# Splitting six PSUM banks two to four between exponential scores and row maxima, with row maxima taken two heads at a time

## The chip, the cores and the metric

The kernel runs on one core of one Trainium2 chip. The metric is the device time of the whole program in microseconds (us). Its engines are PE (matmuls; PEld is its weight load), DVE (vector), ACT (scalar), POOL and SP, each with its own instruction stream, tied together by semaphores.

## The reference

```python
# x: (1, 2048, 128) f32; 16 heads of 8, latent width 64; all operands f32
c_kv   = x @ W_dkv.T
q_lat  = einsum('bqhd,hdl->bhql', (x @ W_dq.T @ W_uq.T).reshape(B, T, 16, 8), k_eff)
attn   = softmax(where(causal, einsum('bhql,bkl->bhqk', q_lat, c_kv) / sqrt(8), -inf))
y      = einsum('bhql,hld->bqhd', einsum('bhqk,bkl->bhql', attn, c_kv), v_eff)
x1     = layernorm(x + y)
# mixture of experts: 2 groups of tokens, 8 experts, top 2, at most 80 tokens each
h      = relu(einsum('egch,ehf->egcf', expert_in, wi)); expert_out = einsum('egcf,efh->egch', h, wo)
out    = layernorm(x1 + combine(expert_out))
```

Causal attention over 2048 tokens and 16 heads comes first and takes most of the time; the experts' work is laid between its pieces.

## The kernel before

**Units and steps.** The queries are cut into 4 supers of 512 and the heads into 4 groups of 4 (HG), which makes 16 units. A unit of super s has 4(s+1) steps (L80): a step takes 128 keys against the 512 queries for the unit's four heads. There are 160 steps. For each head of a step PE computes a transposed tile of scores (keys on the partitions, L1089) into a bank of PSUM, ACT takes the exponential out of it into SBUF (L662), and two steps later PE multiplies the four heads' exponentials with the values into the bank `acc` (`attn_v`, L1106, eight short-weight matmuls a step). The last four steps of a unit lie on the diagonal: they are 512, 384, 256 and 128 queries wide and have one more small matmul (L1093), which adds the mask.

**Maxima.** The exponentials need each row's maximum beforehand. So for a later unit PE also computes tiles the other way round, with queries on the partitions ("items", L1067), and DVE takes the maximum of each. An item is (query tile qt, head h, 512 keys c), in the order of L100. Off the diagonal it is 512 wide and DVE uses TENSOR_REDUCE (L789); the item on the diagonal is (qt+1)*128 wide and DVE adds a mask and takes the maximum in one instruction (L794), followed by a short read of its accumulator. `max_rows` (L797) joins the parts, PE turns the result (L1074), ACT copies it (L638) and a DMA puts it into rows of qT.

**Banks.** PSUM has eight banks. Three (`scT`) are a ring for the exponentials' scores, three (`sc`) a ring for the items, one is `acc`, one `ms` is for turns and the experts. From step WIDE = 140 on there are no items left; then all six ring banks serve the scores, two tiles to one exponential (L660). Score n waits until the exponential that last used its bank is done (L1087); item i waits until item i-3 has been reduced (L1065).

**The order of work.** `woven()` (L119) gives each step its items. It goes backwards from the last item and fills steps up to a limit of work (`item_work`, 60 plus the width, L113; limits 2400 and, for the first 20 steps, 3000), so that a unit's items are done LEAD = 5 steps before the unit begins. A step's items are cut into four gaps. PE's order in one step is: gap 0's items, score 0, gap 1's items, score 1, `attn_v` of two steps before (unless that is a unit's first step, when it comes after gap 3), gap 2's items, score 2, gap 3's items, score 3, and then the step's tasks. All engines execute their own instructions in order. DVE takes the items of a step before that step's other work, and fills some waits with items of the next step.

```
per_step[b].insert(0, i)
...
if early and gap == 2:
    attn_v(due)
for i in gaps[gap]:
    scores_for_max(i)
if b < NSTEP:
    scores(b, gap)
```

**Tasks** (`SCHEDULE`) are the unit's copy of its result `keep_y` (ACT, L673, after the exponentials of the next unit's second step), the turns, layer norms, the router and the experts (`expert_h` L1191, `expert_o` L1197). PE's part of a task stands after score 3 of its step.

Of the kernel before, what the change touches and what calls it, by code (L numbers as in the profile page):

```python
# [26 lines left out]
P = 128  # L27
# [3 lines left out]
QUERIES = 512  # L31
SUPERS = T // QUERIES
TILES = T // P
QT = QUERIES // P
HG = 4
# [6 lines left out]
MROW = 126  # L42
VC = HD + 1
PRING = 12
SRING = 3
AHEAD = 1
EARLY = 16
LEAD = 5
# [3 lines left out]
BIG = -1e38  # L52
# [16 lines left out]
F32, BF16, U32 = mybir.dt.float32, mybir.dt.bfloat16, mybir.dt.uint32  # L69
ALU = mybir.AluOpType  # L70
ACT = mybir.ActivationFunctionType
AX = mybir.AxisListType
# [3 lines left out]
def super_of(u):  # L76
    return u // GROUPS
# [19 lines left out]

def max_items(u):

    return [(qt, h, c) for qt in range(QT) for h in range(HG) for c in range(super_of(u) + 1)]  # L100


ITEMS_BEFORE = [0]
# [4 lines left out]
def max_step(u):  # L108

    return max(0, FIRST[u] - LEAD - 1)  # L110


def item_work(i):  # L113

    u, qt, _, c = ALL_ITEMS[i]
    return 60 + (QUERIES if c < super_of(u) else (qt + 1) * P)


def woven():  # L119

    per_step = [[] for _ in STEPS]
    i, b, work = len(ALL_ITEMS) - 1, FIRST[UNITS - 1], 0
    while i >= ITEMS_BEFORE[AHEAD] + EARLY:
        last = max_step(ALL_ITEMS[i][0])
        limit = ITEM_WORK if b >= RUSH else RUSH_WORK
        if b > last or work + item_work(i) > limit:
            b, work = (b - 1, 0)
            assert b >= 0  # L130
            continue
        per_step[b].insert(0, i)
        work += item_work(i)
        i -= 1
    return [[row[len(row) * gap // 4:len(row) * (gap + 1) // 4] for gap in range(4)] for row in per_step]


# [7 lines left out]
WIDE = max_step(UNITS - 1) + 2  # L145


def score_bank(n):

    return n % SRING if n < HG * WIDE else n % (2 * SRING)  # L150


def used_before(n):

    return max((m for m in range(max(0, n - 4 * SRING), n) if score_bank(m) == score_bank(n)), default=None)


def schedule():
# [87 lines left out]
def program(nc, x_d, wdq_d, wuq_d, wdkv_d, wuk_d, wuv_d, wo_d, router_d, wi_d, wo2_d, out_d):  # L246
    ctx = ExitStack()
    with ctx:
# [12 lines left out]
        qT = [sb(f"qT{i}", [P, HEADS, QUERIES], BF16) for i in range(2)]  # L261
# [47 lines left out]
        causal = sb("causal", [P, QUERIES])  # L309
# [3 lines left out]
        unused = [sb(f"unused{i}", [P, QUERIES], BF16) for i in range(2)]  # L313
        part_max = [sb(f"part_max{i}", [P, QT * HG, SUPERS]) for i in range(2)]
# [38 lines left out]
        back2 = sb("back2", [P, MT, C])  # L353
        ein = back2[:, 0:ST, :]

        ring = ctx.enter_context(nc.psum_tensor("ring", [P, 2 * SRING, QUERIES], F32))
        scT = [ring[:, i, :] for i in range(SRING)]
        sc = [ring[:, SRING + i, :] for i in range(SRING)]
        acc = ctx.enter_context(nc.psum_tensor("acc", [P, QUERIES], F32))
        ms = ctx.enter_context(nc.psum_tensor("ms", [P, QUERIES], F32))  # L360
        BANKS = [*scT, *sc, acc[:, :], ms[:, :]]

        s_w = sem("s_w")
        s_router = sem("s_router")
# [18 lines left out]
        v_kept = sem("v_kept")  # L383
        kq_first = [sem(f"kq_first{g}") for g in range(GROUPS)]
        kq_in = [sem(f"kq_in{i}") for i in range(SUPERS)]
        sc_made = sem("sc_made")
        sc_used = sem("sc_used")
# [33 lines left out]
        def turn_bank(task):  # L421
            return BANKS[bank_of(TURN[task])]

# [301 lines left out]
        def _(dve):  # L725
            made = [0]
            items = [ITEMS_BEFORE[AHEAD], 0]
            may_fill = [False]

            def next_item():  # L730
                row_max(items[0])
                items[0] += 1

            def link(ins):

# [47 lines left out]

            def row_max(i):
                u, qt, h, c = ALL_ITEMS[i]
                dve.wait_ge(sc_made, i + 1)
                dst = part_max[u % 2][:, qt * HG + h, c:c + 1]
                if c < super_of(u):
                    nc.vector.tensor_reduce(dst, sc[i % SRING][:, :], AX.X, ALU.max).then_inc(sc_used, 1)  # L789
                else:  # L790
                    w = (qt + 1) * P
                    if i >= 2:
                        dve.wait_ge(sc_used, i - 1)
                    nc.vector.tensor_tensor_reduce(unused[i % 2][:, 0:w], sc[i % SRING][:, 0:w], causal[:, QUERIES - w:QUERIES], 1.0, 3 * BIG,  # L794
                                                   ALU.add, ALU.max, dst).then_inc(sc_used, 1)

            def max_rows(u):  # L797

# [14 lines left out]
            for u in range(AHEAD):  # L813
                for i in range(ITEMS_BEFORE[u], ITEMS_BEFORE[u + 1]):
                    row_max(i)
                max_rows(u)
            for _ in range(EARLY):
                next_item()

            def moments(rows, kind, k):  # L820
# [192 lines left out]
        def _(pe):  # L1013
# [42 lines left out]
            def scores_for_max(i):  # L1056

                u, qt, h, c = ALL_ITEMS[i]
                s, head = super_of(u), u % GROUPS * HG + h
                if i == ITEMS_BEFORE[u] and s == 0:  # L1060
                    pe.wait_ge(kq_first[u], 16 * 2 * PARTS)
                if i == ITEMS_BEFORE[u] and s and u == s * GROUPS:
                    pe.wait_ge(kq_in[s], 16 * 2 * PARTS)
                if i >= SRING:
                    pe.wait_ge(sc_used, i - SRING + 1)  # L1065
                w = QUERIES if c < s else (qt + 1) * P
                nc.tensor.matmul(sc[i % SRING][:, 0:w], qT[s % 2][0:MROW, head, qt * P:(qt + 1) * P],  # L1067
                                 kT[0:MROW, head, c * QUERIES:c * QUERIES + w], start=True, stop=True).then_inc(sc_made, 1)

            def turn_max(u, bank):  # L1070
# [170 lines left out]
```

## Time and profile before

| what | us |
|---|---|
| median of 3 runs | 589.88 |
| lowest and highest of them | 589.47, 592.38 |
| the profiled execution's own time | 590.35 |
| its span in the profile | 588.5 |
| PE busy | 525.7 (89%) |
| DVE busy | 442.9 (75%) |
| ACT busy | 354.1 (60%) |

The span is what the trace covers; 1.85 us of the profiled execution lie around it. A matmul's row is longer than the time it takes from its successor, since the array is a pipeline: matmuls of one kind follow each other at a shorter pitch than their duration. So PE's "busy" says little about how full PE is; the pitch of its rows says it. Attention runs from about 50 to 522 us; steps with items end at about 482.

### The profile page before, as it was taken

The page shows a single profiled execution, that of the slowest core. Times are in us where ns is not written, and L with a number is a line of the kernel's source. Part 1 is how long each engine was busy: PE and PEld are TensorE (multiplying, and loading weights), DVE is VectorE, ACT ScalarE, POOL GpSimd, SP SyncE. Part 2 cuts the span into 40 slices and gives each one's busy share as a digit, 9 for nine tenths or more (in the row PEclk, how much of TensorE's full clock was granted, in tenths as well). Part 3 has the DMA queues.
Part 4 walks back from the last instruction along what each step waited for, and adds up shares of the span by engine and source line. Part 5 has one row for each costly group of instructions (what it writes and reads, how often), then busy time and mean ns, then how long its engine had stood idle before and what let it go on. Part 6 is the DMA issues. An engine that isn't in the chain of part 4 may idle for free.

```text
span 588.5 us, 10326 instructions
## 1 busy us (share of the span) xinstructions
PE 525.7 (89%) x3491; PEld 217.9 (37%) x3491; DVE 442.9 (75%) x1300; ACT 354.1 (60%) x719; POOL 63.2 (11%) x64
## 2 busy tenths in 40 slices
PE   4967999899999998989989999989999999955991
PEld 2523333233333333224545333333223222223891
DVE  3687999898888979976757878988888872445616
ACT  0613556656667765664765777667777779934231
POOL 9400000000000000450000460000000000000031
PEclk9966999999999999998999999999999999985996
DMA  3379991300000300010000160000000000000024
GB/s 87 120 225 232 200 279 51 58 2 2 2 1 2 82 1 1 29 64 6 1 13 1 37 48 3 1 3 0 1 2 2 1 2 10 19 9 1 0 41 55
DMA packets 25410, 24.90 MB, mean 42 GB/s; under 512 B 2314, under 2 KB 22668, under 8 KB 25356
## 3 DMA queue, kind: packets, MB, share of 16 engines
q1 hardware_dynamic: 21660, 20.42, 13.7%
q0 software_dynamic: 1280, 2.62, 3.8%
q10 hardware_dynamic: 2416, 1.18, 0.7%
q8 instruction: 28, 0.46, 0.3%
q14 instruction: 26, 0.21, 0.1%
HBM read 16.81 MB, written 7.28 MB: 41 GB/s over the span
## 4 chain that ended last, share of the span: by engine, by line
PE 59%; issue 20%; DVE 11%; DMA 3%; POOL 3%; ACT 2%; SPq 0%; ACTq 0%; DVEq 0%; POOLq 0%
PE acc L1106 16%; PE ring L1067 15%; PE ring L1089 13%; DVE part_max L789 3%; POOL exp_in L579 3%; DVE unused L794 2%; PE ring L1093 2%; PE ms L1170 2%; DMA qT<-maxT 1%; PE ms L1197 1%; PE ms L1191 1%; PE ring L1184 1%; PE ring L1197 1%; PE ring L1191 1%; DVE x L865 1%
## 5 line engine op out<-in xcount | busy, mean ns | idle before, releaser
L662 ACT ACTIVATE probs<-ring 128x512 f32<-128x512 f32 (+3 forms) x560 | 268.5, 536 | 136.4 <-PE ring L1093 74.0
L789 DVE TENSOR_REDUCE part_max<-ring 128x1 f32<-128x512 f32 x384 | 254.4, 686 | 45.1 <-PE ring L1067 42.1
L1067 PE MATMUL ring<-kT,qT 126*128 126x512 bf16 (+3 forms) x640 | 221.6, 360 | 10.0 <-DVE part_max L794 4.5
L1089 PE MATMUL ring<-qT,kT 128*128 128x512 bf16 (+3 forms) x640 | 214.5, 352 | 4.0 <-DMA qT<-maxT 3.2
L1106 PE MATMUL acc<-probs,v 128*9 128x512 f32 (+3 forms) x1280 | 147.6, 533 | 0.9 <-ACT yT L673 0.9
L794 DVE CUSTOM_DVE_ANT_0 unused<-ring,causal 128x128 bf16<-128x128 f32 (+3 forms) x256 | 120.3, 483 | 20.3 <-PE ring L1067 18.0
L1067 PEld LDWEIGHTS ring<-kT,qT 126*128 126x128 bf16 x640 | 61.9, 98 | 178.7 <-DVE part_max L789 102.5
L1089 PEld LDWEIGHTS ring<-qT,kT 128*128 128x128 bf16 x640 | 61.9, 99 | 46.7 <-ACT probs L660 15.7
L1093 PE MATMUL ring<-later,ident 128*128 128x128 bf16 x256 | 55.4, 221 | 0.0
L1106 PEld LDWEIGHTS acc<-probs,v 128*9 128x9 f32 x1280 | 19.0, 88 | 50.6 <-issue 25.7
L660 ACT ACTIVATE probs<-ring 128x1024 f32<-128x1024 f32 (+3 forms) x40 | 33.2, 900 | 2.8 <-issue 1.6
L1093 PEld LDWEIGHTS ring<-later,ident 128*128 128x128 bf16 x256 | 25.6, 100 | 19.8 <-issue 0.4
L603 POOL TENSOR_TENSOR res<-res,x 128x512 f32<-128x512 f32 x3 | 3.8, 1268 | 225.3 <-DVEq L845 225.3
L794 DVE DVE_READ_ACCUMULATOR2_ANT part_max<- 128x1 f32 x256 | 21.3, 83 | 0.0
L593 POOL DMA_INDIRECT back<-exp_out,slot_out x16 | 15.3, 954 | 51.1 <-DMA exp_out<-x 46.5
L854 DVE SCALAR_TENSOR_TENSOR nt<-rs 128x2 f32<-128x2 f32 (+1 forms) x12 | 1.9, 160 | 22.7 <-ACT rs L685 22.6
L579 POOL DMA_INDIRECT exp_in<-x,slot_in x16 | 15.7, 982 | 24.1 <-DVE slot_in L926 19.5
L683 ACT ACTIVATE lnv<-mv,eps 128x2 f32<-128x2 f32 (+1 forms) x12 | 3.7, 305 | 23.9 <-DVE mv L827 23.9
L606 POOL IOTA kT<- 128x640 f32 x1 | 0.7, 665 | 141.1 <-PE ring L1093 141.1
L593 POOL DMA_INDIRECT x<-exp_out,slot_out x8 | 7.6, 954 | 70.9 <-DMA exp_out<-x 68.7
L638 ACT ACTIVATE maxT<-ms 8x512 bf16<-8x512 bf16 x16 | 9.3, 579 | 9.3 <-PE ms L1074 9.0
L559 POOL MEMSET kT<- 64x4096 uint32 x4 | 13.9, 3509 | 0.1
(179 smaller groups left out, 341.1 us busy)
## 6 DMA issues: line engine op xcount, KB each, us to landing
kT<-parts_k SPq DMA_DIRECT2D x9, 384.0 KB
qT<-parts_q SPq DMA_DIRECT2D x9, 384.0 KB
wi<-in_L_ffn_wi SPq DMA_DIRECT2D x1, 2048.0 KB, 18.5
parts_k<-wi SPq DMA_DIRECT2D x3, 384.0 KB, 3.6
parts_q<-wi SPq DMA_DIRECT2D x3, 384.0 KB, 4.8
kT<-parts_k SPq DMA_DIRECT2D x12, 96.0 KB
qT<-parts_q SPq DMA_DIRECT2D x12, 96.0 KB
x<-in_L_attn_x ACTq DMA_DIRECT2D x4, 256.0 KB, 4.4
```

What stands on the lines that cost most here:

```text
L559: nc.gpsimd.memset(rows, one_pair).then_inc(s_rows, 1)
L579: pool.indirect_dma_start(exp_in_d[:, :], bass.IndirectOffsetOnAxis(slot_in[:, n:n + 1], 0), x1[:, g * MT + n % MT, :], None).then_inc(sca ...
L593: pool.indirect_dma_start(dst, None, exp_out_d[g][:, :], bass.IndirectOffsetOnAxis(slot_out[:, n:n + 1], 0)).then_inc(gathered[PIECES * g ...
L660: nc.scalar.activation(probs[:, at:at + 2, 0:width], ring[:, bank:bank + 2, 0:width], ACT.Exp).then_inc(exp_done, 2)
L662: nc.scalar.activation(probs[:, at, 0:width], ring[:, bank, 0:width], ACT.Exp).then_inc(exp_done, 1)
L789: nc.vector.tensor_reduce(dst, sc[i % SRING][:, :], AX.X, ALU.max).then_inc(sc_used, 1)
L794: nc.vector.tensor_tensor_reduce(unused[i % 2][:, 0:w], sc[i % SRING][:, 0:w], causal[:, QUERIES - w:QUERIES], 1.0, 3 * BIG, ALU.add, ALU. ...
L1067: nc.tensor.matmul(sc[i % SRING][:, 0:w], qT[s % 2][0:MROW, head, qt * P:(qt + 1) * P], kT[0:MROW, head, c * QUERIES:c * QUERIES + w], sta ...
L1089: ins = nc.tensor.matmul(bank[:, 0:QUERIES - off], kT[:, head, j * P:(j + 1) * P], qT[s % 2][:, head, off:QUERIES], start=True, stop=True, ...
L1093: ins = nc.tensor.matmul(bank[:, 0:P], ident16[:, :], later16[:, :], start=False, stop=True, skip_group_check=True)
L1106: ins = nc.tensor.matmul(acc[32 * h:32 * h + VC, off:QUERIES], v[:, j, head, :], probs[:, (HG * b + h) % PRING, 0:QUERIES - off], start=(j ...
L1170: ins = nc.tensor.matmul(bank[:, 0:n], x1[:, g * MT + i, :], hot[i][:, part * QUERIES:part * QUERIES + n], start=(i == 0), stop=(i == MT - 1))
```

## The change

```diff
-SRING = 3
+SRING = 2
+MRING = 4
+PAIR = 2
 
 def max_items(u):
-    return [(qt, h, c) for qt in range(QT) for h in range(HG) for c in range(super_of(u) + 1)]
+    return [(qt, h + i, c) for qt in range(QT) for h in range(0, HG, PAIR) for c in range(super_of(u) + 1) for i in range(PAIR)]
 
@@ woven
-        per_step[b].insert(0, i)
-        work += item_work(i)
-        i -= 1
+        per_step[b] = [i - 1, i] + per_step[b]
+        work += PAIR * item_work(i)
+        i -= PAIR
 
 def score_bank(n):
-    return n % SRING if n < HG * WIDE else n % (2 * SRING)
+    return n % SRING if n < HG * WIDE else n % (SRING + MRING)
 
@@ banks
-        ring = ctx.enter_context(nc.psum_tensor("ring", [P, 2 * SRING, QUERIES], F32))
-        scT = [ring[:, i, :] for i in range(SRING)]
-        sc = [ring[:, SRING + i, :] for i in range(SRING)]
+        ring = ctx.enter_context(nc.psum_tensor("ring", [P, SRING + MRING, QUERIES], F32))
+        scT = [ring[:, i, :] for i in (0, 1, 5)]
+        sc = [ring[:, SRING + i, :] for i in range(MRING)]
 
@@ row_max, on DVE
-                dve.wait_ge(sc_made, i + 1)
-                dst = part_max[u % 2][:, qt * HG + h, c:c + 1]
                 if c < super_of(u):
-                    nc.vector.tensor_reduce(dst, sc[i % SRING][:, :], AX.X, ALU.max).then_inc(sc_used, 1)
+                    dve.wait_ge(sc_made, i + PAIR)
+                    at = SRING + i % MRING
+                    nc.vector.tensor_reduce(part_max[u % 2][:, qt * HG + h:qt * HG + h + PAIR, c], ring[:, at:at + PAIR, :],
+                                            AX.X, ALU.max).then_inc(sc_used, PAIR)
+                    return PAIR
                 else:
+                    dve.wait_ge(sc_made, i + 1)
+                    dst = part_max[u % 2][:, qt * HG + h, c:c + 1]
                     w = (qt + 1) * P
                     if i >= 2:
                         dve.wait_ge(sc_used, i - 1)
 
@@ scores_for_max, on PE
-                if i >= SRING:
-                    pe.wait_ge(sc_used, i - SRING + 1)
+                if i >= MRING:
+                    pe.wait_ge(sc_used, i - MRING + 1)
+                if i == MRING - 1:
+
+                    pe.wait_ge(v_kept, SUPERS)
```

Not shown: `i % SRING` becomes `i % MRING` where items are written and read, `next_item` counts by what `row_max` returns, `used_before` looks back 2 * (SRING + MRING) = 12 scores as before, and the early loop of DVE runs until the same 16 items are done. The third V tile of the start (`scT[2]`) lies in ring bank 5, which is now also the items' fourth bank; the new wait of item 3 is for that.

The exponentials' scores have two banks instead of three until step 140, the items four instead of three. Two heads' off-diagonal items of the same qt and c stand next to each other, in adjacent banks, and one TENSOR_REDUCE of 2 x 512 takes both maxima; it waits for both tiles and frees both banks when it ends. The diagonal items keep an instruction each. `woven()` places items in twos, so that a step has an even number of them: evaluated, the new plan has 2, 4, 6 or 8 items in a step, and none in steps 0, 3, 11 to 13, 19, 43, 44, 55, 56, 91, 92, 107, 108, 123 and 124; the old one has 3 or more in nearly every step below 139. With R for an off-diagonal item, 1 to 4 for a diagonal one of that many 128 columns, and | between the gaps, the pattern of steps 113 to 124 is:

```
step  before     after
113   2|R|R|R    R|R2|2|RR
114   2|R|R|R2   R|RR|R|22
115   R|R|R|3    R|R|R|R
116   R|R|R|3    R|R|3|3
117   R|R|R|3    R|R|R|R
118   R|R|R|3    R|R|3|3
119   R|R|R|4    R|R|R|R
120   R|R|R|4    R|R|4|4
121   R|R|R|4    R|R|R|R
122   R|R|R|4    R|R|4|4
123   |R|R|R     |||
124   1|R|R|R    |||
127   1|R|R|R    R|RR|R|11
```

## Rows read from the trace of the kernel before

**Rows 1.** The page: busy time of the engines, and two of its costliest groups
```profile
PE 525.7 (89%) x3491; PEld 217.9 (37%) x3491; DVE 442.9 (75%) x1300; ACT 354.1 (60%) x719; POOL 63.2 (11%) x64
...
L789 DVE TENSOR_REDUCE part_max<-ring 128x1 f32<-128x512 f32 x384 | 254.4, 686 | 45.1 <-PE ring L1067 42.1
L1067 PE MATMUL ring<-kT,qT 126*128 126x512 bf16 (+3 forms) x640 | 221.6, 360 | 10.0 <-DVE part_max L794 4.5
```

**Rows 2.** The chain of work that ended last, 405 to 450 us, by line
```profile
by line: PE acc L1106 32.5%; PE ring L1067 32.3%; PE ring L1089 26.6%; DVE part_max L789 4.5%; PE ring L1093 1.6%; DVE unused L794 0.9%; PE ms L1074 0.9%; issue 0.8%; DVE max L810 0.2%; DVE part_max L794 0.0%
```

**Rows 3.** The timeline of one regular step, 117: start us, us, instruction, idle before
```profile
417.30 0.39 PE L1067 MATMUL ring<-kT,qT 126*128 126x512 bf16 x1
...
417.52 0.38 PE L1089 MATMUL ring<-qT,kT 128*128 128x512 bf16 x1
...
417.72 0.69 DVE L789 TENSOR_REDUCE part_max<-ring 128x1 f32<-128x512 f32 x1 [0.41 <-PE ring L1067]
...
417.91 0.38 PE L1089 MATMUL ring<-qT,kT 128*128 128x512 bf16 x1
...
417.94 2.07 ACT L662 ACTIVATE probs<-ring 128x512 f32<-128x512 f32 x4 [0.71 <-PE ring L1089]
...
418.34 0.38 PE L1089 MATMUL ring<-qT,kT 128*128 128x512 bf16 x1
...
418.78 0.38 PE L1089 MATMUL ring<-qT,kT 128*128 128x512 bf16 x1
...
419.09 1.05 PE L1106 MATMUL acc<-probs,v 128*9 128x512 f32 x8
...
420.07 0.39 PE L1067 MATMUL ring<-kT,qT 126*128 126x512 bf16 x1
```

**Rows 4.** Groups by form, whole span: count, busy us, mean ns, idle before
```profile
L662 ACT ACTIVATE probs<-ring 128x512 f32<-128x512 f32 x392 | 208.8, 601 | 84.3 <-PE ring L1089 58.8 <-PE ring L1093 23.1 <-PE acc L1106 1.2
...
L794 DVE CUSTOM_DVE_ANT_0 unused<-ring,causal 128x512 bf16<-128x512 f32 x64 | 42.8, 683 | 4.3 <-PE ring L1067 3.9 <-DVE res L840 0.3
...
L662 ACT ACTIVATE probs<-ring 128x384 f32<-128x384 f32 x56 | 26.1, 496 | 14.8 <-PE ring L1093 14.5
...
L794 DVE CUSTOM_DVE_ANT_0 unused<-ring,causal 128x128 bf16<-128x128 f32 x64 | 17.6, 283 | 6.9 <-PE ring L1067 6.3 <-DVE res L840 0.3
```

**Rows 5.** The timeline where a unit begins, steps 113 and 114
```profile
409.85 0.38 PE L1089 MATMUL ring<-qT,kT 128*128 128x512 bf16 x1
410.00 0.60 ACT L673 ACTIVATE yT<-acc 128x512 f32<-128x512 f32 x1
...
410.42 1.88 DVE L789 TENSOR_REDUCE part_max<-ring 128x1 f32<-128x512 f32 x3
410.44 0.38 PE L1089 MATMUL ring<-qT,kT 128*128 128x512 bf16 x1
410.48 2.08 ACT L662 ACTIVATE probs<-ring 128x512 f32<-128x512 f32 x4
...
411.16 0.10 PEld L1067 LDWEIGHTS ring<-kT,qT 126*128 126x128 bf16 x1 [0.51 <-DVE part_max L789]
...
411.28 0.38 PE L1089 MATMUL ring<-qT,kT 128*128 128x512 bf16 x1
```

**Rows 6.** The timeline of a step with an expert's matmuls behind score 3
```profile
300.40 0.38 PE L1089 MATMUL ring<-qT,kT 128*128 128x512 bf16 x1
...
300.62 1.01 PE L1191 MATMUL ms<-einT,wi 128*128 128x80 f32 x8
...
301.53 0.38 PE L1089 MATMUL ring<-qT,kT 128*128 128x512 bf16 x1
```

**Rows 7.** Who waited for whom, whole span: us in total, times, longest
```profile
PEld ring L1067 <- DVE part_max L789: 102.5, 180, 1.4
...
PE ring L1067 <- DVE part_max L794: 4.5, 8, 2.6
...
PE ring L1067 <- DVE part_max L789: 3.7, 10, 0.9
...
PE ms L1164 <- DMA back<-exp_in: 2.7, 1, 2.7
```

**Rows 8.** Stretches: us, busy us of the engines, granted clock, DMA share, GB/s
```profile
60.00:100.00 40.00, 38.02 (x295) 15.51 (x294) 37.88 (x129) 23.20 (x58) 0.00 (x0) 1.00 0.72 178
...
250.00:300.00 50.00, 47.18 (x321) 20.77 (x318) 34.69 (x83) 31.20 (x65) 8.73 (x9) 0.97 0.08 24
...
400.00:450.00 50.00, 49.44 (x327) 15.91 (x327) 42.39 (x96) 35.91 (x78) 0.00 (x0) 1.00 0.00 1
```

More of the change, by code:

```diff
@@ L148, in score_bank @@
 def score_bank(n):
-    return n % SRING if n < HG * WIDE else n % (2 * SRING)
+    return n % SRING if n < HG * WIDE else n % (SRING + MRING)
 def used_before(n):
-    return max((m for m in range(max(0, n - 4 * SRING), n) if score_bank(m) == score_bank(n)), default=None)
+    return max((m for m in range(max(0, n - 2 * (SRING + MRING)), n) if score_bank(m) == score_bank(n)), default=None)
 def schedule():
@@ L354, in program @@
         ein = back2[:, 0:ST, :]
-        ring = ctx.enter_context(nc.psum_tensor("ring", [P, 2 * SRING, QUERIES], F32))
-        scT = [ring[:, i, :] for i in range(SRING)]
-        sc = [ring[:, SRING + i, :] for i in range(SRING)]
+        ring = ctx.enter_context(nc.psum_tensor("ring", [P, SRING + MRING, QUERIES], F32))
+        scT = [ring[:, i, :] for i in (0, 1, 5)]
+        sc = [ring[:, SRING + i, :] for i in range(MRING)]
         acc = ctx.enter_context(nc.psum_tensor("acc", [P, QUERIES], F32))
         ms = ctx.enter_context(nc.psum_tensor("ms", [P, QUERIES], F32))
-        BANKS = [*scT, *sc, acc[:, :], ms[:, :]]
+        BANKS = [*scT[0:SRING], *sc, acc[:, :], ms[:, :]]
         s_w = sem("s_w")
@@ L730, in next_item @@
             def next_item():
-                row_max(items[0])
-                items[0] += 1
+                items[0] += row_max(items[0])
             def link(ins):
@@ L793, in row_max @@
                         dve.wait_ge(sc_used, i - 1)
-                    nc.vector.tensor_tensor_reduce(unused[i % 2][:, 0:w], sc[i % SRING][:, 0:w], causal[:, QUERIES - w:QUERIES], 1.0, 3 * BIG,
+                    nc.vector.tensor_tensor_reduce(unused[i % 2][:, 0:w], sc[i % MRING][:, 0:w], causal[:, QUERIES - w:QUERIES], 1.0, 3 * BIG,
                                                    ALU.add, ALU.max, dst).then_inc(sc_used, 1)
+                    return 1
             def max_rows(u):
@@ L816, in _ @@
                 max_rows(u)
-            for _ in range(EARLY):
+            while items[0] < ITEMS_BEFORE[AHEAD] + EARLY:
                 next_item()
@@ L1063, in scores_for_max @@
                     pe.wait_ge(kq_in[s], 16 * 2 * PARTS)
-                if i >= SRING:
-                    pe.wait_ge(sc_used, i - SRING + 1)
+                if i >= MRING:
+                    pe.wait_ge(sc_used, i - MRING + 1)
+                if i == MRING - 1:
+                    pe.wait_ge(v_kept, SUPERS)
                 w = QUERIES if c < s else (qt + 1) * P
-                nc.tensor.matmul(sc[i % SRING][:, 0:w], qT[s % 2][0:MROW, head, qt * P:(qt + 1) * P],
+                nc.tensor.matmul(sc[i % MRING][:, 0:w], qT[s % 2][0:MROW, head, qt * P:(qt + 1) * P],
                                  kT[0:MROW, head, c * QUERIES:c * QUERIES + w], start=True, stop=True).then_inc(sc_made, 1)
```

## The prediction

> **What bounds the kernel now.** I read the page first: PE is busy 89% of the span, DVE 75%, ACT 60% [rows 1]. A full PE row can hide waits, so the chain comes next. Over one whole unit it runs through PE for over nine tenths and through DVE's maxima for 4.5 + 0.9 = 5.4% [rows 2]: PE streams, and DVE is seldom late. Then the timeline of one step [rows 3]. The matmul before a score starts at 417.30 and the score at 417.52, so a 512-column matmul takes 0.22 of PE though its row says 0.38. The four scores between two attn_v's (call them S1 to S4; they are scores 2 and 3 of one step and 0 and 1 of the next, and I call this a cluster) start at 417.52, 417.91, 418.34 and 418.78; attn_v begins at 419.09 and the next step's first item at 420.07. The step is 2.77 us, with no hole for PE. The ring of three score banks is what makes this possible, and the row of ACT shows by how much.
>
> **The score ring, three banks to two.** Score n may now start when exponential n-2 is done, not n-3. The first exponential starts at 417.94, 0.42 after S1 starts, and lasts 0.60 [rows 3, 4]: it ends at 418.54. Four of them take 2.07, so they follow each other at (2.07 - 0.60)/3 = 0.49. From the end of a releasing instruction to PE's next start there is 0.05: of three maxima that take 1.88 from 410.42 at 0.69 for the last, the first ends at 411.11, and the load that waited for it starts at 411.16 [rows 5]. I take 0.06 with the matmul behind the load. So S3 can't start before 418.60, and it started at 418.34: a stall of 0.26. Exponential 2 starts at 418.43 and ends at 419.03, so S4 can't start before 419.09; shifted with S3 it would come at 419.04: 0.05 more. A regular cluster with four wide items costs about 0.3, and S1 and S2 cost nothing, since attn_v's 0.98 stands before them. The same sum for other clusters of the new plan, always (0.42 + 0.60 + 0.06 = 1.08) against what stands between S1 and S3 at 0.22 a wide matmul and 0.054 for each 128 columns of a narrow one:
> - 46 clusters below step 139 between two full-width steps, 4 to 6 items, no task behind score 3: 30 x 0.28 + 9 x 0.23 + 7 x 0.10 = 11.2 us.
> - 5 such with only 2 or 3 items, next to an empty step: 0.68 each, 3.4 us. 5 between two empty steps (S1 to S4 would take 0.65, and need 1.56; the maxima's turn fills some 0.25): 0.61 each, 3.0 us.
> - 38 with diagonal steps: their exponentials are shorter (0.50 at 384 [rows 4]) and the masks fill: 0.18 each, 6.8 us.
> - Some 45 with a task of PE behind score 3. An expert's eight matmuls put 1.13 between S2 and S3 [rows 6] (300.40 to 301.53), above the 0.6 that is missing at most: nothing. If these tasks were not there, they would pay as the others do.
> Together 24 us. Bounds: with no release delay at all S3's stall is 0.20, which makes 18; with every stall also delaying what comes behind, 30.
>
> **At a unit's start** attn_v is missing in the middle of one step and ACT's copy of the result (L673) stands between exponentials. There S5 started at 410.44, and the exponential two before it ends at 410.48 + 0.60 = 411.08 [rows 5]: 0.70 short instead of 0.28. Eleven units pay this 0.42 more: 5 us; from 2 (the old stall for DVE at 411.16 lies in the same place) to 8.
>
> **The pairs on DVE.** 384 instructions become 192 [rows 1]. Off two singles at a pitch of 0.60 (1.88 for three), 1.29 us, one of 1024 elements is not in the trace. Between the L794 rows 384 more columns cost 683 - 283 = 400 ns [rows 4], 0.133 for 128, so 512 more cost 0.53 and a pair lasts 0.69 + 0.53 = 1.22; from 0.69 (the second half free) to 1.37 (nothing saved). At 1.22 DVE gets back 0.07 a pair, 13 us of work, of which PE feels what it waited for DVE. PE's own rows show 4.5 + 3.7 = 8 us of waits for maxima [rows 7]; the chain's 5.4% of 45 us is 2.4 a unit, 27 us over eleven units if all of it were regained. I take 8, the waits that are seen, with 5 and 28 as ends. The 102.5 us of loads that waited [rows 7] are not a price: they lie beside attn_v.
>
> **The pairs on PE.** A pair must be whole before it is reduced, and frees two banks only at its end. With four banks item i waits for item i-4. In the pattern R|R|R|R a pair lies within gaps 0 and 1, or 2 and 3, and nothing is late. In R|RR|R|11, R|RR|R|22 and 2|2R|R|33 a pair has its first tile before attn_v and its second behind. From attn_v's end: the second tile starts, its reduce starts 0.42 later [rows 3] (417.30 to 417.72), lasts 1.22, and PE hears 0.05 after: 1.69. PE wants that bank for the first item of the next step after item, score, two narrow items, score: 0.22 + 0.22 + 0.11 + 0.22 = 0.77. That is 0.9 of stall, 0.8 with 22. The score stall of the same cluster (0.3) is inside it. The new plan has 31 such steps; 12 have a task behind score 3 and are reached late enough (together some 2.5 us), the other 19 add about 0.65 each, 12.3; three of them are a unit's third step, where attn_v comes elsewhere: -1.6. Together 13 us, from 6 (pairs nearer 0.69) to 22. The Trainium skill, in Perfetto Trace Analysis, Optimizing Scalar/DVE Operations, says that where DVE is not saturated but makes others wait, breaking instructions up lets work end sooner. By that rule the merging costs time even where it saves DVE work, as in the 13 us here. The same section says that grouping helps an engine that is saturated; by that the merging would bring up to 13 us instead. The trace, with DVE at 42.39 of 50 us [rows 8] and PE seldom waiting for it, agrees with the first.
>
> **Edits at nothing.** A diagonal maximum behind a pair now waits for the pair's end (0.05 to 0.1, some 90 times): DVE has 15% free, and would cost up to 9 us without it. The wait of item 3 for the V copies lies at the start, where DVE still splits k and q and the fourth item waited for it anyway. After step 140 the banks are as before. The 16 empty steps are paid above; their items make others fuller, and in the first 20 steps, where DVE is busy 37.88 of 40 us [rows 8], they leave DVE idle and then press it: 0 to 4 us.
>
> **The sum.** 24 + 5 + 13 - 8 = +34. On the profiled execution (590.35, of which 588.5 are the span) that is 624.4; it lies 0.5 above the median of the runs, so I say 624.
>
> **Rivals.** (A) The straddling pairs cost little, because DVE takes them early enough or the stall falls into the score stall: 24 + 5 - 8 = +21, 611. For: DVE's idle time before L789 is 45 us, almost all of it for PE [rows 1], so it starts at once. Against: the 0.77 against 1.69. (B) DVE decides: each maximum saved shortens the step wherever DVE sets the pace, and PE's queue swallows the score stalls. Then -13 us, 577. For: DVE's 37.88 of 40 in the early stage. It decides from the point where DVE's work for a step is longer than PE's; for four wide items it is 4 x 0.60 = 2.4 against 2.77 [rows 3], so hardly anywhere. (C) The third bank is slack: ACT's exponentials keep up and the kernel stays at 590 +- 3. Against: exponential n-2 ends after score n starts, in the row itself. (D) The clock. So far the granted clock is 1.00 (2.4 GHz) in the stages with items, and 0.97 in 250 to 300 [rows 8], where PE once stood for 2.7 us [rows 7]. If the new regular stalls of 0.3 in 3 us pulled it down in one step of ten, 14 steps would take up to 2.8 more: 39 on top, 663. The stage of 60 to 100, with PE waiting for DVE time and again, kept 1.00. The Trainium skill, TensorE: Matmul & The Clock Gate, A second HAM failure mode, tells of a kernel whose short idles at its PSUM banks made the clock go up and down; the trace does not show it for waits of this length.
>
> **How the numbers follow.** Forecast 0.60, A 0.24, D 0.05, B 0.05, C 0.06. The range takes the forecast's bounds, from 590 + 18 + 2 + 6 - 20 = 596 to 590 + 30 + 8 + 22 - 5 = 645; all low ends together are unlikely, so 603 to 645, which holds A and leaves out B, C and D. A measurement of this kernel tells about 0.5% from no change. Slower by more: 0.60 + 0.24 + 0.05 and a small part of C, 0.90; faster 0.05; the same 0.05.
>
> **What would show it.** The regular step at about 3.07 us instead of 2.77 where items are R|R|R|R, with PE's load for L1089 released by ACT's exponential; steps with R|RR|R|11 at about 3.8 with the load for L1067 released by L789; L789 192 times at 1.2 us; DVE's busy time lower by some 13 us; ACT's busy time unchanged. The span from step 140 on should be unchanged. The prediction is wrong if S3 starts less than 0.42 + 0.60 after S1 with full-width tiles, if L1067 does not wait in straddling steps, or if the clock falls between 60 and 480 us.

## The result and the profile after

The changed kernel takes 644.39 us (median of 4 runs, 642.21 to 646.77) beside 589.69 for the kernel before on the same chip: a ratio of 1.0931, 95% interval 1.0907 to 1.0956. It is slower, by 54.7 us where +34 was forecast; 644.39 lies just inside the range's upper end of 645. The profiled execution took 644.41, with a span of 642.7.

The page of the changed kernel, against [rows 1]:

```profile
PE 538.7 (84%) x3491; PEld 214.8 (33%) x3491; DVE 439.0 (68%) x1108; ACT 364.6 (57%) x719; POOL 63.1 (10%) x64
...
L790 DVE TENSOR_REDUCE part_max<-ring 128x2 f32<-128x1024 f32 x192 | 232.2, 1223 | 91.0 <-PE ring L1076 89.9
L1076 PE MATMUL ring<-kT,qT 126*128 126x512 bf16 (+3 forms) x640 | 211.5, 360 | 31.2 <-DVE part_max L790 26.3
L1098 PE MATMUL ring<-qT,kT 128*128 128x512 bf16 (+3 forms) x640 | 216.6, 355 | 18.9 <-ACT probs L664 11.2
```

PE and ACT execute as many instructions as before, and DVE fewer. PE's and ACT's busy time is 13.0 and 10.5 us longer all the same, in part because rows that follow each other at once overlap and fewer do so now: four exponentials of 0.60 took 2.07 in a run before, and take 2.17. What grew is waiting in both directions: DVE stood 91.0 us before its maxima where it was 45.1, and PE 26.3 us before an item, for DVE's pairs, where it was 3.7. Two engines that wait more for each other, with the same work, have lost slack between them. The waits say the same, against [rows 7] (first the changed kernel, then the rows of the kernel before that [rows 7] has not):

```profile
PEld ring L1076 <- DVE part_max L790: 77.4, 99, 1.6
PEld ring L1098 <- ACT probs L664: 76.3, 155, 2.1
...
PE ring L1076 <- DVE part_max L790: 26.3, 44, 1.2
...
PE ms L1153 <- DVE x L871: 7.5, 3, 2.6
...
PE ms L1083 <- DVE max L816: 6.1, 5, 2.8
```

```profile
PEld ring L1089 <- ACT probs L662: 4.0, 10, 0.9
...
PE ms L1144 <- DVE x L865: 3.6, 3, 1.2
...
PE ms L1074 <- DVE max L810: 2.5, 3, 1.9
```

The second row of the changed kernel is the score ring: the load for a score waits for an exponential 155 times, where it did so 10 times. Its last two have nothing to do with banks: PE waits up to 2.8 us for a layer norm (`x`) and for the finished maxima (`max`), in all 13.6 us where it was 6.1. The chain of waits from 450 to 500 us, about one unit like that of [rows 2], has the maxima at 15.8% where they had 4.5, and ACT at 6.1% where it had no entry:

```profile
by line: PE acc L1115 26.0%; PE ring L1098 22.6%; PE ring L1076 21.2%; DVE part_max L790 15.8%; ACT probs L664 6.1%; issue 5.8%; ACTq L645 1.3%; ACT maxT L640 0.9%; PE ring L1102 0.9%; DVE unused L799 0.5%; DVE part_max L799 0.3%; DVEq L788
```

**A regular step**, R|R|R|R, on the timeline; this answers [rows 3]:

```profile
457.42 1.04 PE L1115 MATMUL acc<-probs,v 128*9 128x512 f32 x8
...
458.62 0.38 PE L1098 MATMUL ring<-qT,kT 128*128 128x512 bf16 x1
...
459.04 2.17 ACT L664 ACTIVATE probs<-ring 128x512 f32<-128x512 f32 x4 [0.87 <-PE ring L1098]
...
459.69 0.10 PEld L1098 LDWEIGHTS ring<-qT,kT 128*128 128x128 bf16 x1 [0.53 <-ACT probs L664]
459.69 0.39 PE L1098 MATMUL ring<-qT,kT 128*128 128x512 bf16 x1
...
460.18 0.39 PE L1098 MATMUL ring<-qT,kT 128*128 128x512 bf16 x1
...
460.50 1.05 PE L1115 MATMUL acc<-probs,v 128*9 128x512 f32 x8
```

S1 starts at 458.62, S3 at 459.69: 1.07 apart, where the forecast had 1.08. S4 follows at the exponentials' pitch, and attn_v comes 3.08 after the last (forecast 3.07, before 2.77). **A crowded step** of the pattern R|RR|R|11:

```profile
442.50 0.38 PE L1076 MATMUL ring<-kT,qT 126*128 126x512 bf16 x1
...
442.60 2.36 DVE L790 TENSOR_REDUCE part_max<-ring 128x2 f32<-128x1024 f32 x2 [0.37 <-PE ring L1076]
...
443.88 0.39 PE L1076 MATMUL ring<-kT,qT 126*128 126x512 bf16 x1 [0.67 <-DVE part_max L790]
...
444.31 0.83 PE L1115 MATMUL acc<-probs,v 128*9 128x384 f32 x8
...
445.58 1.23 DVE L790 TENSOR_REDUCE part_max<-ring 128x2 f32<-128x1024 f32 x1 [0.62 <-PE ring L1076]
...
446.86 0.39 PE L1076 MATMUL ring<-kT,qT 126*128 126x512 bf16 x1 [1.05 <-DVE part_max L790]
```

The pair that straddles attn_v begins at 445.58, and the item that needs its bank waits 1.05 us for the end of it. That wait was foreseen (0.9). The one at 443.88 was not: two pairs stand in a row on DVE, and PE reaches the bank of the first while it is still being reduced. From its first item to that of the next step this one takes 4.36 us, and 1.72 of them are the two waits. It is not the forecast's own case, though: it is the last step of a unit, its own scores are 128 wide and take PE little time, so PE comes to each bank early. Steps 95, 111 and 127 are of this kind. In step 36 (R|RR|R|22, scores 512 wide) the trace has the one foreseen wait, 0.62 us long at 182.44, and the step takes 4.06.

Where in the kernel does the time go? By the start of a step's first score in the two traces, the changed kernel is 0.7 us ahead at step 4, then behind by 3.9 at step 20, 19.9 at step 48, 34.1 at step 96 and 53.5 at step 140, and it stays at 53.5 to the end. So nearly all of it comes before the last step with items, some 0.4 us a step from step 20 on. (The new plan has 4, 6, 8 or 10 items in a step that has any: 10 in steps 1 and 4, and in none only 2.)

### The profile page after: what moved, and what is told of

The parts are those of the page before. It is cut to its first block, busy times and chain, and to the rows that moved or that the text cites. A ratio compares the mean times of both kernels' runs of the same rounds, so it can differ in the third digit from the quotient of the medians.

```text
span 642.7 us, 10324 instructions
## 1 busy us (share of the span) xinstructions
PE 538.7 (84%) x3491; PEld 214.8 (33%) x3491; DVE 439.0 (68%) x1108; ACT 364.6 (57%) x719; POOL 63.1 (10%) x64
## 4 chain that ended last, share of the span: by engine, by line
PE 49%; issue 23%; DVE 16%; ACT 5%; DMA 3%; POOL 3%; ACTq 1%; SPq 0%; DVEq 0%; POOLq 0%
PE acc L1115 14%; PE ring L1098 12%; PE ring L1076 11%; DVE part_max L790 9%; POOL exp_in L581 2%; ACT probs L664 2%; PE ms L1179 2%; DMA qT<-maxT 1%; PE ms L1206 1%; PE ms L1200 1%; DVE unused L799 1%; PE ring L1193 1%; PE ring L1102 1%; PE ring L1206 1%; PE ring L1200 1%
## 5 line engine op out<-in xcount | busy, mean ns | idle before, releaser
L664 ACT ACTIVATE probs<-ring 128x512 f32<-128x512 f32 (+3 forms) x560 | 277.9, 532 | 173.2 <-PE ring L1102 88.6
L790 DVE TENSOR_REDUCE part_max<-ring 128x2 f32<-128x1024 f32 x192 | 232.2, 1223 | 91.0 <-PE ring L1076 89.9
L1076 PE MATMUL ring<-kT,qT 126*128 126x512 bf16 (+3 forms) x640 | 211.5, 360 | 31.2 <-DVE part_max L790 26.3
L799 DVE CUSTOM_DVE_ANT_0 unused<-ring,causal 128x128 bf16<-128x128 f32 (+3 forms) x256 | 115.0, 488 | 29.2 <-PE ring L1076 17.7
L1076 PEld LDWEIGHTS ring<-kT,qT 126*128 126x128 bf16 x640 | 59.9, 99 | 169.5 <-DVE part_max L790 77.4
L860 DVE SCALAR_TENSOR_TENSOR nt<-rs 128x2 f32<-128x2 f32 (+1 forms) x12 | 1.9, 160 | 23.6 <-ACT rs L687 23.5
## 6 DMA issues: line engine op xcount, KB each, us to landing
wi<-in_L_ffn_wi SPq DMA_DIRECT2D x1, 2048.0 KB, 19.9
```

Source lines behind the costliest of these rows:

```text
L664: nc.scalar.activation(probs[:, at, 0:width], ring[:, bank, 0:width], ACT.Exp).then_inc(exp_done, 1)
L790: nc.vector.tensor_reduce(part_max[u % 2][:, qt * HG + h:qt * HG + h + PAIR, c], ring[:, at:at + PAIR, :], AX.X, ALU.max).then_inc(sc_used ...
L1076: nc.tensor.matmul(sc[i % MRING][:, 0:w], qT[s % 2][0:MROW, head, qt * P:(qt + 1) * P], kT[0:MROW, head, c * QUERIES:c * QUERIES + w], sta ...
```

## The experiments

Differences of medians are given in us. The interval of each ratio reaches 0.2 to 0.5% to either side, 1 to 3 us, and the runs come from three chips, on which the kernel before took 589.6, 589.5 and 588.8. So a difference between two of these kernels is known to 3 or 4 us.

**1. Banks, plan and merging apart.** In the first kernel only the banks are new (2 and 4), with the old order and one maximum at a time:

```diff
-    return [(qt, h + i, c) for qt in range(QT) for h in range(0, HG, PAIR) for c in range(super_of(u) + 1) for i in range(PAIR)]
+    return [(qt, h, c) for qt in range(QT) for h in range(HG) for c in range(super_of(u) + 1)]
-        per_step[b] = [i - 1, i] + per_step[b]
+        per_step[b].insert(0, i)
@@ row_max
-                    dve.wait_ge(sc_made, i + PAIR)
-                    at = SRING + i % MRING
-                    nc.vector.tensor_reduce(part_max[u % 2][:, qt * HG + h:qt * HG + h + PAIR, c], ring[:, at:at + PAIR, :],
-                                            AX.X, ALU.max).then_inc(sc_used, PAIR)
-                    return PAIR
+                    dve.wait_ge(sc_made, i + 1)
+                    nc.vector.tensor_reduce(part_max[u % 2][:, qt * HG + h, c:c + 1], sc[i % MRING][:, :], AX.X, ALU.max).then_inc(sc_used, 1)
+                    return 1
```

> Only the banks are split two to four; the plan of the items and their single maxima are those of the kernel before. Theory (the score ring is the main cost, with the pairs that straddle attn_v second): +24 for the clusters of the old plan, +5 at unit starts, little back from a fourth item bank: 615 to 620 us, the regular step 3.07 us instead of 2.77. Rival (the third score bank is slack, the merging costs all): 588 to 592. Second rival (the score ring costs the whole of it): 640 or more.

Measured: 605.98, ratio 1.0278 (1.0230 to 1.0326), +16. That is between the theory and its first rival, and neither had it: the third score bank is not slack, but it costs 16 of the 29 expected.

The second has only the new order and plan, with three and three banks and single maxima (the changed kernel with the lines below and the diff above in `row_max`, and without the new wait of item 3):

```diff
-SRING = 2
-MRING = 4
+SRING = 3
+MRING = 3
-        scT = [ring[:, i, :] for i in (0, 1, 5)]
+        scT = [ring[:, i, :] for i in range(3)]
```

> Only the order and the plan of the items in twos, with banks three and three and a maximum for each item. Theory: the empty steps cost little while there are three score banks, 590 to 598 us. Rival (the plan's empty and crowded steps are where the 20 us come from by which the changed kernel is slower than forecast): 605 to 612.

Measured: 608.01, 1.0323 (1.0277 to 1.0369), +18, as the rival had it. Its regular step is nearly as before (2.82 from one attn_v to the next). Its waits show a part of the 18 us: PE waits for DVE 35 times where [rows 7] has 10, 6.8 us more in all:

```profile
PE ring L1071 <- DVE part_max L789: 10.5, 35, 1.1
```

Another part lies in the 16 empty steps. There PE has only scores and attn_v, and even with three banks the load for a score waits for an exponential 25 times, 15.4 us in all by the trace, where the kernel before has 8 such waits, 2.6 us, in all its steps below 139. Some of that lies beside attn_v, so it is not a price, and the 18 us were not divided further.

The third is the changed kernel with nothing undone but the merging, that is, with the diff in `row_max` above and nothing else.

> The changed kernel with each off-diagonal maximum taken by an instruction of its own; banks and plan stay as changed. Theory: the straddling pairs fall away and no item waits for its neighbour: 644 less 13 to 25, so 619 to 631; a step with R|RR|R|11 at about 3.2 us instead of 3.6 to 4.4. Rival (the merging saves DVE time and is not what costs): 644 to 655.

Measured: 612.57, 1.0399 (1.0356 to 1.0442), +23, below the 619 to 631 of the theory: the merging costs more than I thought. Of the 54.7 us, banks and plan together make 23 and **the merging 31.8**. In this kernel's waits PE's own row for the maxima is as small as before:

```profile
PE ring L1074 <- DVE part_max L789: 3.9, 15, 0.8
```

The plan costs 18 with banks three and three and only 6.6 more (612.57 - 605.98) with two and four, where PE's waits for DVE fall from 10.5 to 3.9. Read the other way, the banks cost 16 in the old plan and 4.6 (612.57 - 608.01) in the new one. That the fourth item bank is what cushions the crowded plan fits those rows. It may also be that the stalls of the one hide in those of the other. No run had 2 and 3 banks with the new plan, so both are argued and not shown.

**2. Is the fourth item bank of use in the old plan?** Two score banks, three item banks and one idle, with the old order and single maxima (`MRING = 3` and `SPARE = 1` in the first kernel).

> Two banks for the scores as changed, but three for the items as before (the eighth bank idle), plan and single maxima as before: the score ring alone. The split of banks cost 16 where 29 had been forecast. Theory (the fourth item bank gives some of the difference back, as fewer waits for DVE): 609 to 615 us. Rival (the fourth item bank is worth nothing and the score ring costs only 16): 604 to 607.

Measured: 606.56, 1.0291 (1.0261 to 1.0321), 0.6 from the first kernel, which is the rival's result. No worth of the fourth item bank can be told there; the 17 us are the score ring alone. Its timeline has the stall in its pure form:

```profile
429.58 1.04 PE L1111 MATMUL acc<-probs,v 128*9 128x512 f32 x8
...
431.85 0.10 PEld L1094 LDWEIGHTS ring<-qT,kT 128*128 128x128 bf16 x1 [0.58 <-ACT probs L665]
...
432.33 0.10 PEld L1094 LDWEIGHTS ring<-qT,kT 128*128 128x128 bf16 x1 [0.37 <-ACT probs L665]
...
432.66 1.05 PE L1111 MATMUL acc<-probs,v 128*9 128x512 f32 x8
```

Again 3.08 from attn_v to attn_v, with DVE in no way involved.

**3. The straddling pairs.** If the merging costs time because a pair lies on both sides of attn_v, keeping it whole must give that back. First with both tiles behind attn_v, R|R|RR|11:

```diff
+    cut = [len(row) * gap // 4 for gap in range(5)]
+    if cut[2] % PAIR:
+        u, _, _, c = ALL_ITEMS[row[cut[2]]]
+        if c < super_of(u):
+            cut[2] -= 1
+    return [row[cut[gap]:cut[gap + 1]] for gap in range(4)]
```

> The changed kernel with one cut moved: an off-diagonal pair is never divided by attn_v (R|RR|R|11 becomes R|R|RR|11). Theory: the 19 steps in question regain about 0.65 us each and those with a task a little: 644 less 10 to 20, so 624 to 634. Rival (a pair costs by its length wherever it stands): 642 to 646.

Measured: 638.23, 1.0829 (1.0784 to 1.0875), only 6.2 below the changed kernel: less than the theory's 10 to 20, and more than the rival's nothing. Then with both ahead of it, R|RRR||11, so that attn_v covers the reduction:

```diff
-            cut[2] -= 1
+            cut[2] += 1
+            cut[3] = max(cut[2], cut[3])
```

> The changed kernel with the divided pair put whole ahead of attn_v (R|RR|R|11 becomes R|RRR||11), so that it is reduced beside attn_v. The run before put it whole behind attn_v and gained 6 us. Theory (what costs is that the pair ends 1.7 us behind attn_v while the next step's first item wants its bank): most crowded steps go from 3.6-4.4 to 3.0-3.3 us, 644 less 12 to 20, so 624 to 632. Rival (a pair costs by being two tiles long wherever it stands, DVE then being late for the next one): 636 to 642.

Measured: 634.23, 1.0776 (1.0737 to 1.0816), 10.2 below, between the theory's 12 and the rival's 8. PE's waits for pairs fall from 26.3 to

```profile
PE ring L1087 <- DVE part_max L801: 17.3, 33, 1.2
```

So the straddling is real and costs about what was forecast (13, of which 10 come back). But two thirds of the 31.8 are somewhere else.

**4. The pairs as fills.** `link()` on DVE puts an item's maximum between two short instructions that depend on each other. A single maximum there is 0.69 long and waits for one tile; a pair is 1.22 long and waits for two. The changed kernel's DVE in the last instructions of a layer norm, on which PE's turn (L1153) waits:

```profile
419.89 0.16 DVE L860 SCALAR_TENSOR_TENSOR nt<-rs 128x4 f32<-128x4 f32 x1
419.96 1.22 DVE L790 TENSOR_REDUCE part_max<-ring 128x2 f32<-128x1024 f32 x1
421.10 0.16 DVE L861 TENSOR_TENSOR nt<-nt,var 128x4 f32<-128x4 f32 x1
421.90 1.23 DVE L790 TENSOR_REDUCE part_max<-ring 128x2 f32<-128x1024 f32 x1 [0.65 <-PE ring L1076]
423.04 0.15 DVE L862 SCALAR_TENSOR_TENSOR rs<-nt,rs 128x4 f32<-128x4 f32 x1
423.23 1.12 DVE L871 TENSOR_SCALAR x<-res,mv,rs 128x128 f32<-128x128 f32 x4
```

L861 done, DVE sits 0.65 us in a fill whose second tile PE hasn't made, though L862 could run. In the experiment only diagonal items, which kept an instruction each, may fill:

```diff
-                if may_fill[0] and items[0] < items[1]:
+                u, _, _, c = ALL_ITEMS[min(items[0], len(ALL_ITEMS) - 1)]
+                if may_fill[0] and items[0] < items[1] and c == super_of(u):
```

> The changed kernel in which DVE fills the waits of its chained small operations with a diagonal item only, never with a pair. Theory (each filled wait now takes 1.22 us and waits for two tiles, so the chains of the layer norms end late and PE's turns with them): steps 57, 58, 105 and 106 regain 1 to 1.5 us each, 644 less 4 to 8, so 636 to 640. Rival (the fills cost nothing, the chain's PE turns were late anyway): 643 to 646.

Measured: 635.00, 1.0789 (1.0750 to 1.0829), 9.4 below the changed kernel where 4 to 8 were expected. The same instructions:

```profile
414.64 0.16 DVE L861 SCALAR_TENSOR_TENSOR nt<-rs 128x4 f32<-128x4 f32 x1
414.83 0.16 DVE L862 TENSOR_TENSOR nt<-nt,var 128x4 f32<-128x4 f32 x1
415.02 0.16 DVE L863 SCALAR_TENSOR_TENSOR rs<-nt,rs 128x4 f32<-128x4 f32 x1
415.22 1.11 DVE L872 TENSOR_SCALAR x<-res,mv,rs 128x128 f32<-128x128 f32 x4
```

and PE's waits for that output:

```profile
PE ms L1154 <- DVE x L872: 0.2, 1, 0.2
```

From L861 (L860 in the other) to the start of the norm's output at L872 it is 0.58 us instead of 3.34, and of the 7.5 us that PE waited 0.2 are left. A part of the gain is the clock. In the changed kernel PE stood 2.58, 2.40 and 2.48 us before its three turns of a norm's output, at 142.09, 250.81 and 424.49. The three stretches of 50 us that hold these turns have a granted clock of 0.97, and behind the last of them a 512-column matmul's row lasts 0.63 us where it is 0.39 elsewhere. Without pairs as fills the stretches from 250 to 300 and from 400 to 450 have 1.00, and only 100 to 150 still has 0.97. The control is the kernel before with the same restriction, since there the fills are singles:

> Control: the kernel before with the same restriction on fills (only diagonal items, each off-diagonal maximum being a single of 0.69 us). Theory (single fills are short, and what they save in idle time they cost in the chain): 588 to 592. Rival (fills are harmful by themselves, merged or not): under 587.

Measured: 588.03, 0.9981 (0.9954 to 1.0008): no change that can be told. The fill is harmless with the singles of the old plan and harmful with pairs. Both cures together (pairs ahead of attn_v, no pair as a fill):

> Both edits of the two runs before together. Theory (two separate costs of the merged instruction): the gains add up, 644 less 16 to 28, so 616 to 628, near the 612.6 of the kernel without merging. Rival (they are the same stalls seen twice): no better than the better of the two.

Measured: 626.10, 1.0639 (1.0590 to 1.0687), 18.3 below the changed kernel beside 10.2 + 9.4 = 19.6 for each alone. Within what the runs can tell, the two are separate and add up. To the kernel without merging 13.5 us are still missing.

**5. Is the rest the crowded steps?** My theory then was that pairs are free where every step has exactly four items, so that no step is crowded. The plan gets limits that make it so from step 32 to 138; the steps before 32 get up to 10 items:

```diff
-ITEM_WORK = 2400
-RUSH, RUSH_WORK = 20, 3000
+ITEM_WORK = 2090
+RUSH, RUSH_WORK = 32, 3500
```

once in the changed kernel (pairs), once in the kernel without merging (singles).

> The changed kernel with another limit in the plan: from step 32 on every step has exactly four items, no step is empty and no pair is divided by attn_v; the surplus goes into steps 20 to 31, with up to eight items. Theory (merging costs only where pairs meet crowded steps): from the first score of step 32 to that of step 140 it takes 341 to 346 us (328.3 before, 370.6 changed), and the whole kernel 618 to 630, by what steps 20 to 31 lose. Rival (a merged maximum costs wherever it stands): 355 or more for that stretch.

> The same plan of fours with a maximum for each item (the kernel without merging, other limit). Theory: the stretch from step 32 to 140 within 3 us of the merged one of the same plan, so the merge is free there; the whole kernel 610 to 620. Rival: 10 us or more faster than the merged one in that stretch.

Measured: 640.34, 1.0853 (1.0807 to 1.0898) with pairs, 616.56, 1.0459 (1.0428 to 1.0491) with singles. The theory failed: the merging costs 23.8 us in this plan too. For its main stretch I had expected 341 to 346 us with pairs and at most 3 less with singles. Scores are missing in these two traces, so I take attn_v: from the attn_v of step 30 to that of step 138 the pairs take 354.4 and the singles 339.6. Nearly all of the difference lies behind step 48: from its attn_v to that of step 140 the pairs take 305.9 and the singles 291.5, and the 14.3 between them are made up by eleven of the 92 intervals from one attn_v to the next, at or just behind steps in which DVE has a chain of its own (a norm, `top2`, the finished maxima). The other 9 or so come before step 32, where this plan is crowded. One of the eleven, with pairs:

```profile
482.32 0.22 DVE L812 TENSOR_REDUCE neg_max<-part_max 128x16 f32<-128x64 f32 x1
...
482.56 1.23 DVE L790 TENSOR_REDUCE part_max<-ring 128x2 f32<-128x1024 f32 x1
...
483.70 0.16 DVE L815 CAST max<-neg_max 128x16 bf16<-128x16 f32 x1
...
484.56 1.23 DVE L790 TENSOR_REDUCE part_max<-ring 128x2 f32<-128x1024 f32 x1 [0.70 <-PE ring L1076]
485.70 0.17 DVE L816 TENSOR_TENSOR max<-neg_max,max 128x16 bf16<-128x16 f32 x1
...
486.01 0.38 PE L1083 MATMUL ms<-ident,max 128*8 128x128 bf16 x4 [1.34 <-DVE max L816]
```

and with singles:

```profile
459.30 0.22 DVE L810 TENSOR_REDUCE neg_max<-part_max 128x16 f32<-128x64 f32 x1
...
459.44 0.68 DVE L789 TENSOR_REDUCE part_max<-ring 128x1 f32<-128x512 f32 x1
...
460.04 0.17 DVE L813 CAST max<-neg_max 128x16 bf16<-128x16 f32 x1
460.11 0.69 DVE L789 TENSOR_REDUCE part_max<-ring 128x1 f32<-128x512 f32 x1
...
460.71 0.17 DVE L814 TENSOR_TENSOR max<-neg_max,max 128x16 bf16<-128x16 f32 x1
...
461.58 0.39 PE L1081 MATMUL ms<-ident,max 128*8 128x128 bf16 x4
```

From `neg_max` to `max` it is 3.38 with pairs and 1.41 with singles, and PE, which needs `max` behind score 3, stands 1.34 us in the one and not at all in the other. At the turns of two norms it stands 2.48 with pairs and 1.24 with singles. So this plan shows what the pairs cost in DVE's chains, clean of the crowded steps. The plan of fours with no pair as a fill was not tried.

**6. Is there something to win before?** In the kernel before, only the norms' output is taken out of the tasks that may be filled (`FILLED` without `"norm_out"`):

> The kernel before, with no items filled into the chained operations of the layer norms' last part alone (the control that kept off-diagonal items out of all chains came out at a ratio of 0.998). Theory (PE's turn of x1 waits for that chain at three places, 0.5 to 1 us each): 587 to 589, a ratio of 0.996 to 0.999. Rival (the items that are not filled are late for PE instead): 589.5 or more.

Measured: 588.49, 0.9995 (0.9975 to 1.0016). No change that can be told. No version here beats the kernel before.

## Why the prediction was right in direction and short in size

**The score ring** (24 + 5 at unit starts). Right in mechanism to a few hundredths: the load for S3 released by the exponential, 1.07 between S1 and S3, the step at 3.08. Banks and plan together measured +23 for 29 forecast, inside 18 + 2 to 30 + 8. But the size came out near by luck. The 29 was a price for the banks, and in the new plan they cost only 4.6 on top of the plan's 18; in the old plan they cost 17 alone. There the trace of the kernel with two, three and one idle shows which parts were sized well, interval by interval from one attn_v to the next. From step 20 on, the 41 with full-width scores and no task of PE cost 0.25 each, near the 0.28 of the forecast, and the 28 with a task next to nothing, 0.7 together. But the 30 with diagonal steps cost 0.06 each where the forecast had 0.18, and the 20 beside a unit's start 3.0 together, where the forecast had 5 for the starts on top of the clusters. What I had at "0 to 4 us" for the empty steps, outside the sum, is, together with the fuller steps that the plan makes elsewhere, worth +18 when the plan stands alone.

**The pairs: +13 on PE, -8 on DVE, so +5. This is the step that failed; it measured +31.8.** Three things were in it.

- The straddling term was sound: 10.2 of the forecast 13 come back when pairs stand whole ahead of attn_v. Yet I counted one wait in such a step and took its scores as 512 wide. In steps 95, 111 and 127, whose scores are 128 wide, the trace shows two, of 0.67 and 1.05.
- The fills were missing altogether: 9.4 us. The prediction named DVE's fills nowhere. It asked who waits for the tiles' banks, and not who waits for the short DVE instructions behind a pair. The code said that maxima stand between them, and in the kernel before PE already waited 3.6 us for the norms' output and 2.5 for the finished maxima; a fill of twice the length, which also waits for a tile more, had to be priced.
- The -8 for DVE was regained nowhere. The instruction came as estimated: 192 of 1223 ns for 1.22, and against the kernel without merging its busy row falls from 244.7 to 232.2, the 13 us that I worked out; DVE in all is only 3.8 us less busy (442.8 to 439.0). The rest is overlap: the rows of the maxima lie over other rows of DVE for 15.4 us without merging and for 6.2 with it, so that much of the 13 was never time of its own. And its idle time before the maxima rose by 46 us against [rows 1]. Work was taken from an engine that wasn't short of time, and its latency was raised, which the others feel.

That leaves 31.8 - 18.3 = 13.5 us of the merging. In the kernel with both cures the waits still have 20.2 us of PE for pairs beside 3.9 in the kernel without merging. Where they lie, the two timelines show: from the attn_v of step 0 to that of step 138 the pairs lose 13.6 us, 12.8 of it in intervals that touch a step with six or more items and 0.8 in the 71 that touch only steps with four or none. So the rest is in the crowded steps. That it is pairs in a row there, as at 443.88, is argued and not shown.

That 644.39 still lies in the range is luck too. The range's upper end added the high ends of the ring (38 for 29) and of the pairs (22 - 5 = 17). The ring with the plan took 23, and the pairs 31.8, well beyond their own end: what the one left over paid for the other. (In the low end DVE's gain was entered as 20 where the text has 28; no reading here rests on it.)

**The rivals.** A (+21, the straddle is cheap) fell: it isn't cheap, and there was more. B (DVE decides, -13) fell by the same runs: less DVE work made the kernel slower. C (the third bank is slack) fell with the first experiment. D, the clock falling, came true in a small part, and not by the stalls that it named:

```profile
100.00:150.00 50.00, 40.04 (x266) 14.96 (x265) 37.29 (x110) 27.09 (x56) 1.27 (x1) 0.97 0.12 25
...
400.00:450.00 50.00, 43.52 (x267) 14.65 (x259) 34.93 (x84) 29.23 (x60) 1.27 (x1) 0.97 0.00 1
430.00:480.00 50.00, 45.70 (x277) 12.83 (x277) 36.44 (x70) 32.95 (x65) 0.00 (x0) 1.00 0.01 1
```

These are the changed kernel's stretches (columns as in [rows 8]): the granted clock is 0.97 in two of them, where the kernel before has 1.00, and 1.00 in the last, which is full of regular stalls of 0.3 us. The two are stretches in which PE stood 2.6 and 2.5 us for a norm. That is the prediction's sign "if the clock falls between 60 and 480 us", but by my estimate small: 0.03 of 50 us is 1.5 us in each. The mean is 0.958 beside 0.956 before, so the clock doesn't explain the 54.7. The rule of the Trainium skill's TensorE: Matmul & The Clock Gate, A second HAM failure mode, which had short idles at PSUM banks switch the clock up and down, is not what these stalls did: 430 to 480 has 1.00.

Of the two rules on grouping in the Trainium skill's Perfetto Trace Analysis, Optimizing Scalar/DVE Operations, this case bears out the one for an engine that isn't saturated and makes others wait: with DVE 72% busy (442.8 of 613.1), 192 instructions in place of 384 cost 31.8 us. The other, grouping for throughput, made the row of the maxima 12.5 us shorter and DVE's busy time 3.8, and PE's waits for DVE grew.

**The other signs.** Right: the regular step, the crowded step's wait on L790, the 1.22, no difference from step 140 on. Wrong: DVE's busy time (-3.9 for -13), ACT's (354.1 to 364.6 where it should not change), the clock in two stretches, and the crowded step, 4.06 and 4.36 us for 3.8 in the two read here.

## What to carry to other kernels

A ring's depth is priced by one round trip: from the producer's start over the consumer's start and length to the release, here 0.42 + 0.60 + 0.05, set against what the producer does between two uses of the same slot; for a regular step that arithmetic came out to 0.01 us. How many steps are regular is another question, and there the forecast was off. Merging two instructions on an engine that is not the bound is a change of latency, not of throughput: list every place where the merged instruction may stand, the fills between short dependent instructions too, and ask at each who is waiting behind it. A bank moved from one ring to another is worth only what the receiving ring was short of, which in the old plan was nothing that could be told. And two changes priced apart need not add up: here the banks cost 16 or 17 us under one plan and 4.6 under the other.

## What the runs showed of the hardware that I had not expected

- **The reduction of two tiles** costs DVE 1.22 us alone and 1.13 when they follow each other (two take 2.36 at 442.60), beside 0.69 and 0.60 for one. Merging saves 0.07 us a pair, and where both tiles are there the first bank comes free 0.53 later than it would.
- **The same kernel differs by 1% with its mean granted clock.** The five runs of the kernel with pairs ahead of attn_v took 640.3, 634.2, 634.8, 634.1 and 634.0 us at clocks of 0.946, 0.959, 0.956, 0.959 and 0.962, and its profile is the first of them. Those 6 us are as much as separates some of the variants, so they are compared by medians here, and from that profile only waits are read.
- **Waits that PE shows are a poor measure of what they cost.** The kernel with no pair as a fill is 9.4 us faster than the changed one, and its PE stands longer for the pairs (30.7 us in its waits, beside 26.3): what it no longer waits for at the norms it waits for in part at the banks.
- **The clock fell where PE stood for some 2 us, and not in stalls of 0.3 us.** The three waits of 2.40 to 2.58 us for a norm's output lie in the three stretches at 0.97. Without pairs as fills the one stretch left at 0.97, 100 to 150, has a wait of 1.85 us for an exponential (at 136.17). From 430 to 480, with a stall of 0.3 us in every 3 us, it stayed at 1.00.
